# A two-layer graph network: one tile of gathered rows in each round is fetched row by row by SyncE and ScalarE

## The reference, cut to what matters

```python
def _L0_gnn_ref(feat, W1, W2, b, src, dst):
    t1 = feat @ W1
    msg = t1[src] + feat[src] * feat[dst] @ W2
    msg = msg / (sqrt(out_deg[src]) * sqrt(out_deg[dst]))[:, None]
    agg = segment_sum(msg, dst)
    embed = leaky_relu(where(in_cnt[:, None] > 0, t1 + agg, 0) + b, 0.01)
    return embed / maximum(norm(embed), 1e-12)

def _L1_gnn_ref(x, W, b, edge_index):
    xt = einsum('ni,oi->no', x, W) + b
    return segment_sum(xt[src], tgt) / (deg + 1.0)[:, None]

x = _layernorm(x + _L0_gnn_ref(x, W1, W2, b0, src, dst))
x = _layernorm(x + _L1_gnn_ref(x, W, b1, edge_index))
```

## Time and profile before

| | |
|---|---|
| median of three runs | 3954.75 us |
| the profiled execution, its span | 3955.7 us |
| GpSimd busy | 2958.4 us (75%) |
| TensorE busy, by overlapping records | 3009.0 us (76%) |
| VectorE busy | 1854.3 us (47%) |
| ScalarE busy | 671.9 us (17%) |
| layer 0, first to last gather's start | 372.2 to 1979.4 us |
| layer 1, first to last gather's start | 2004.5 to 3935.1 us |

### The profile page before, as it was taken

How to read it: one execution, slowest core, us unless ns; L and a number is a source line. 1 busy time by engine, 2 the same in 40 slices (tenths; PEclk the granted TensorE clock), 3 DMA queues, 4 the chain that set the end, 5 groups by cost and what they waited for, 6 DMA issues and landing times.

```text
span 3955.7 us, 56274 instructions
## 1 busy us (share of the span) xinstructions
PE 3009.0 (76%) x10186; PEld 1878.7 (47%) x10186; DVE 1854.3 (47%) x3529; ACT 671.9 (17%) x2118; POOL 2958.4 (75%) x3112
## 2 busy tenths in 40 slices
PE   4551887888877778788877888878788878877787
PEld 4441565655556656566534344434444434433443
DVE  9994455555555555555432323233333233323333
ACT  8991111111111111111100000000000000000000
POOL 7776777777777777777757777777777777777776
PEclk5555788888888888887857666677767777677767
DMA  7878455555555555555434444444444444444443
GB/s 254 269 236 318 134 159 158 155 159 160 156 158 158 160 156 160 157 165 157 135 89 118 121 123 122 122 122 122 121 121 121 123 122 121 121 122 122 122 121 107
DMA packets 306368, 588.12 MB, mean 149 GB/s; under 512 B 65107, under 2 KB 189178, under 8 KB 306170
## 3 DMA queue, kind: packets, MB, share of 16 engines
q0 software_dynamic: 148416, 405.47, 35.1%
q1 hardware_dynamic: 144986, 168.09, 12.7%
q10 hardware_dynamic: 12768, 12.85, 0.9%
HBM read 506.24 MB, written 75.45 MB: 147 GB/s over the span
## 4 chain that ended last, share of the span: by engine, by line
POOL 66%; issue 23%; POOLq 1%; DMA 1%; DVE 0%; DVEq 0%; PE 0%; ACT 0%; SPq 0%; ACTq 0%
POOL ring L585 66%; POOLq L582 0%; DMA ring<-scaled_x,idx 0%; DVEq L808 0%; DMA ring<-x,idx 0%; POOLq L583 0%; PE banks L1264 0%; POOL ring L595 0%; DMA x<-out_t 0%; DVE stats L1039 0%; POOLq L627 0%; DMA result<-out_t 0%; DVE out_t L1051 0%; ACT scal L738 0%; POOLq L96 0%
## 5 line engine op out<-in xcount | busy, mean ns | idle before, releaser
L1264 PE MATMUL banks<-ring,hot_space 128*128 128x257 f32 x6252 | 2399.0, 512 | 728.3 <-DMA ring<-x,idx 363.4
L1264 PEld LDWEIGHTS banks<-ring,hot_space 128*128 128x128 f32 x6252 | 1298.5, 238 | 1744.6 <-DMA ring<-x,idx 966.8
L585 POOL DMA_INDIRECT ring<-x,idx x1540 | 1462.1, 949 | 493.7 <-issue 469.2
L585 POOL DMA_INDIRECT ring<-scaled_x,idx x1270 | 1221.2, 962 | 396.5 <-issue 393.7
L970 DVE SCALAR_TENSOR_TENSOR big<-banks,here_mask,big 128x257 f32 x784 | 343.3, 479 | 1693.6 <-PE banks L1264 1693.6
L926 DVE TENSOR_TENSOR hot_space<-banks,dst_rel 128x1024 f32<-128x1024 f32 x392 | 479.6, 1225 | 181.8 <-issue 180.0
L708 ACT COPY idx<-src_col 128x8 int32 (+1 forms) x392 | 77.2, 197 | 2238.8 <-PE banks L1264 2238.8
L595 POOL DMA_INDIRECT ring<-in_x,src_col x276 | 264.9, 960 | 84.1 <-issue 84.1
L671 ACT ACTIVATE dst_rel<-columns,halves 128x128 bf16<-128x128 f32 x960 | 268.3, 375 | 4.6 <-DVE halves L843 4.6
L1163 PE MATMUL banks<-hot_space 128*128 128x98 bf16 x1088 | 101.2, 282 | 132.2 <-DVE hot_space L815 132.2
L1229 PE MATMUL banks<-w_s,a_t 128*128 128x256 f32 x784 | 195.7, 406 | 0.0
(11 more groups left out here) (121 smaller groups left out, 1169.6 us busy)
## 6 DMA issues: line engine op xcount, KB each, us to landing
src_lo<-x SPq DMA_DIRECT2D x2944, 1.0 KB
kept_rows<-ring SPq DMA_DIRECT2D x94, 384.0 KB, 3.2
ring<-kept_rows SPq DMA_DIRECT2D x47, 768.0 KB, 6.0
ring<-x,idx POOLq DMA_INDIRECT x1540, 2.8
src_lo<-scaled_x SPq DMA_DIRECT2D x1408, 1.0 KB
ring<-scaled_x,idx POOLq DMA_INDIRECT x1270, 2.8
dst_col<-in_src SPq DMA_DIRECT2D x47, 384.0 KB, 6.7
scaled_x<-big ACTq DMA_DIRECT2D x14, 896.0 KB, 17.3
```

The source lines that it names most:

```text
L585: g.indirect_dma_start(ring[:, u, 0:D], None, table[layer], bass.IndirectOffsetOnAxis(ap=idx[:, u:u + 1], axis=0)).then_inc(rows_in[u], 16)
L1264: last = nc.tensor.matmul(group_sum(k % SUMS), dst_hot[:, k % HOTS, u - k * GT, :], ring[:, u, 0:DW], start=u == tiles[0], stop=u == tiles ...
```

## The change

Both layers now treat the rounds 2 to 47 alike: GpSimd leaves out the last tile in each of them, 92 times in all where it was 34. SyncE fetches the tile of the even rounds (2h) and ScalarE that of the odd ones (2h+1), 23 each in a layer, each over the two rounds before. SyncE's two parts of 32 rows a round now stand one behind the other, ahead of the loads and stores. ScalarE gets in each round 24, 24 and 16 rows (`ACT_ROWS`), behind the index copies 0, 1 and 2 and, for the first, behind the roots; in every second round it hands the tile over after `scale_kept`. The 48 x 128 source numbers that this needs are loaded once, VectorE shifts them to byte offsets, and they are stored in `row_bytes`. The row's DMA then takes the register as it is, from the table seen as bytes.

```diff
-HANDS = (ROUNDS - 1) // 2
-SPAN = 4
-FEW = (ROUNDS - 1) // SPAN - 1
+HANDS = (ROUNDS - 3) // 2
 HAND_U = U - 1
 HAND_ROWS = 32
+ACT_ROWS = (24, 24, 16)
+ROW_BYTES = 4 * D
...
+        def one_row(layer, start):
+            return table[layer].bitcast(U8).rearrange("n (a b) -> a (n b)", a=1)[:, bass.ds(start, ROW_BYTES)]
...
+            sp.dma_start(hand_sources, src[0:(ROUNDS - 1) * U * P].rearrange("(i t e) -> i t e", t=U, e=P)[:, HAND_U, :]
+                         ).then_inc(sources_in, 16)
...
+            sp.wait_ge(ints_made, 2)
+            sp.dma_start(row_bytes, hand_sources).then_inc(ints_stored, 16)
...
             def load_hand_src(layer, h):
-                i = 2 * h + 1 if layer else SPAN * h
-                sp.dma_start(hand_src, src[bass.ds((i * U + HAND_U) * P, P)].rearrange("(a n) -> a n", a=1)
-                             ).then_inc(hand_src_in, 16)
+                sp.dma_start(hand_src[0], row_bytes[bass.ds(2 * h, 1), :]).then_inc(hand_src_in[0], 16)
...
-                for n, row in enumerate(rows):
-                    sp.dma_start(hand_rows[first + n:first + n + 1, :],
-                                 table[layer][bass.ds(row, 1), :]).then_inc(hand_in[layer], 16)
+                for n, start in enumerate(starts):
+                    sp.dma_start(hand_rows[0][first + n:first + n + 1, :].bitcast(U8),
+                                 one_row(layer, start)).then_inc(hand_in[0][layer], 16)
...
                 if hand is not None:
-                    if part == 0:
+                    if half == 0:
                         hand_free(layer, hand - 1)
-                    hand_part(layer, hand, part, load_next)
+                    hand_part(layer, hand, 2 * half)
+                    hand_part(layer, hand, 2 * half + 1, load_next)
                 next_pair(layer, i - 1)
...
+                    with g.Fori(LOOP_FIRST, ROUNDS - 1) as i:
+                        for q in range(4):
+                            gather_quarter(layer, i, q, HAND_U, 0 if layer else KEPT)
...
+            def hand_part(layer, hand, half, q, load_next):     # on ScalarE
+                if half == 0 and q == 0:
+                    act.wait_ge(hand_src_in[1], 16 * hand_no(layer, h))
+                    act.wait_ge(hand_over[1], 16 * (hand_no(layer, h) - 1))
+                first = half * P // 2 + sum(ACT_ROWS[:q])
+                _, starts = nc.values_load_multi_w_load_instructions(
+                    hand_src[1][:, first:first + ACT_ROWS[q]], engines=[mybir.EngineType.Activation], ...)
+                for n, start in enumerate(starts):
+                    nc.scalar.dma_start(hand_rows[1][first + n:first + n + 1, :].bitcast(U8),
+                                        one_row(layer, start)).then_inc(hand_in[1][layer], 16)
...
+            def pass_hand(layer, h):                             # on ScalarE
+                act.wait_ge(hand_in[1][layer], 16 * P * h)
+                act.wait_ge(groups_done, group_no(layer, 2 * h, GR - 1) + 1)
+                nc.scalar.dma_start(ring[:, HAND_U, 0:D], hand_rows[1].bitcast(F32)).then_inc(hand_over[1], 16)
...
                 if with_kept:
                     scale_kept(i)
+                if passed is not None:
+                    pass_hand(layer, passed)
                 for q in range(4):
...
                     refill(layer, i, q)
                     if ended and q == 0:
                         roots(layer, i - 2)
+                    if hand is not None and q < len(ACT_ROWS):
+                        hand_part(layer, hand, half, q, half == 1 and q == len(ACT_ROWS) - 1 and ...)
...
-                    with act.Fori(2, ROUNDS - 1) as i:
-                        round_(layer, i, True, True, layer == 0)
+                    with act.Fori(1, HANDS) as h:
+                        round_(layer, 2 * h, True, True, layer == 0, hand=h, half=1)
+                        round_(layer, 2 * h + 1, True, True, layer == 0, hand=h + 1, passed=h)
...
+            nc.vector.tensor_scalar(hand_sources, hand_sources, ROW_BYTES.bit_length() - 1, None,
+                                    ALU.logical_shift_left).then_inc(ints_made, 1)
```

More of the change, by code:

```diff
@@ new lines, in _ @@
+                    hand_part(layer, 1, 0)
+                    hand_part(layer, 1, 1)
+                    middle_round(layer, 1, with_kept, with_kept, 1, 1, True)
+                    pass_hand(layer, 1)
+                    with sp.Fori(1, HANDS - 1) as h:
+                        middle_round(layer, 2 * h, with_kept, with_kept, h + 1, 0)
+                        middle_round(layer, 2 * h + 1, with_kept, with_kept, h + 1, 1, True)
+                        pass_hand(layer, h + 1)
+                    middle_round(layer, 2 * HANDS - 2, with_kept, with_kept, HANDS, 0)
@@ L749, in scale_kept, with load_hand_src, hand_part, round_ @@
                 last.then_inc(kept_scaled, 1)
-            def round_(layer, i, sums, ended, with_kept=False, last=False):
+            def load_hand_src(layer, h):
+                nc.scalar.dma_start(hand_src[1], row_bytes[bass.ds(2 * h + 1, 1), :]).then_inc(hand_src_in[1], 16)
+            def hand_part(layer, h, half, q, load_next):
+                if half == 0 and q == 0:
+                    act.wait_ge(hand_src_in[1], 16 * hand_no(layer, h))
+                    act.sem_inc(act_turn, 1)
+                    act.wait_ge(hand_over[1], 16 * (hand_no(layer, h) - 1))
+                    act.sem_inc(act_turn, 1)
+                first = half * P // 2 + sum(ACT_ROWS[:q])
+                _, starts = nc.values_load_multi_w_load_instructions(
+                    hand_src[1][:, first:first + ACT_ROWS[q]], engines=[mybir.EngineType.Activation], min_val=0,
+                    max_val=(NODES - 1) * ROW_BYTES,
+                    skip_runtime_bounds_check_because="a source is a node's number, as for the gathers")
+                if load_next:
+                    load_hand_src(layer, h + 1)
+                for n, start in enumerate(starts):
[3 more added lines that the diff above has]
+                act.wait_ge(hand_in[1][layer], 16 * P * h)
+                act.sem_inc(act_turn, 1)
+                act.wait_ge(groups_done, group_no(layer, 2 * h, GR - 1) + 1)
+                act.sem_inc(act_turn, 1)
+                nc.scalar.dma_start(ring[:, HAND_U, 0:D], hand_rows[1].bitcast(F32)).then_inc(hand_over[1], 16)
+            def round_(layer, i, sums, ended, with_kept=False, last=False, hand=None, half=0, passed=None):
                 if with_kept:
                     scale_kept(i)
+                if passed is not None:
+                    pass_hand(layer, passed)
                 for q in range(4):
@@ L765, in round_ @@
                         roots(layer, i - 2)
+                    if hand is not None and q < len(ACT_ROWS):
+                        hand_part(layer, hand, half, q, half == 1 and q == len(ACT_ROWS) - 1
+                                  and not (isinstance(hand, int) and hand == HANDS))
             act.wait_ge(flag_made, 1)
@@ L1238, in find_places, with round_ @@
                 last.then_inc(places_found, 1)
-            def round_(layer, i, finish, end=U, with_kept=False, find=False, last_one=False):
+            def round_(layer, i, finish, end=U, with_kept=False, find=False, last_one=False, over=None, h=0):
                 for k in range(GR):
```

138 lines of the change are left out of this document (50 added, 88 removed).

## The result

The changed kernel takes **4450.7 us**, the median of four runs (4449.22 to 4453.37), where the kernel before took 3955.48 us beside it: a ratio of 1.1253, 95% interval 1.1239 to 1.1266. It is 495 us slower. The forecast was 4715 us, in a range of 4250 to 5050.

What follows compares the result with a forecast made beforehand. GpSimd's gathers bound the kernel before; the change was to shift the bound to a closed loop through ScalarE's in-order queue. 3956 + 621 (layer 0) + 138 (layer 1) = 4715 us, range 4250 to 5050.

Steps and rivals of the forecast that it cites:

- index copy 3 to copy 0: ScalarE's layer 0 loop: scaling the kept tiles and TensorE's first group, 7.3 us before clock, hand-over and jump.
- copy 0 to the second root: ScalarE's layer 0 loop: existing waits for VectorE around the roots, which nothing makes shorter, 7.0 us.
- reads, 64 rows, copies 1 and 2 and the clearing: ScalarE's layer 0 loop: offset reads 4.4 us, row issue 21.8 us, copies and clearing 0.5 us.
- `a_t` to copy 3: End of ScalarE's layer 0 loop: two a_t copies and the step to copy 3, 1.4 us.
- A row's cost: ScalarE's queue: issuing one row with byte offsets takes 0.34 us, bounds 0.27 and 0.415 us.
- the first rival: ScalarE's queue keeps up and GpSimd stays the bound: 3883 us, needing 0.16 us a row; chance 0.09.
- the second, 0.17 to 0.26: Rows on ScalarE cost 0.17 to 0.26 us, so it bounds layer 0 alone: 4060 us at 0.22; chance 0.05.
- the clock's price: Layer 0: after TensorE's idle wait, products and first group run at a lower clock, 2.5 us a round, bounds 0 to 5.7.
- Hand-over and jump: ScalarE's loop: hand-over DMA with waits, offset load and loop jump back add 1.2 us a round.
- Layer 1, +138 us: ScalarE's loop makes a layer 1 round 42.5 us against 39.5, over 46 rounds; round bounds 38.9 and 45.2.
- SyncE's load: SyncE's own work, 61 us per pair of layer 0 rounds, stays covered by ScalarE's 92 us.
- That issuers hinder each other: Rival: two issuers hinder each other or offsets gain nothing, 0.415 us a row: 5157 us; chance 0.05.

Runs made afterwards that it cites:

- the run with 32 rows: The changed kernel with ScalarE issuing 32 rows a round (16, 8, 8) in place of 64, half its tiles' rows left stale: 3894.93 us.
- the run with layer 1 alone: The changed kernel with ScalarE's tiles in layer 1 only, SyncE's tiles kept in both layers: 3906.49 us, ratio 0.9895 to the kernel before.
- the run with its tiles alone: The changed kernel without ScalarE's rows in both layers; SyncE keeps its 46 tiles, GpSimd gathers the odd rounds' tiles: 3937.11 us, ratio 0.9965.

## Why the prediction was right, and where its sum was too high

**The mechanism held.** ScalarE's loop bounds layer 0, for the reasons given. Step by step, forecast against the round shown above:
- index copy 3 to copy 0: 7.3 us, which is 11.0 with 2.5 for the clock and 1.2 for hand-over and jump; measured 9.07.
- copy 0 to the second root: 7.0 us; measured 6.89.
- reads, 64 rows, copies 1 and 2 and the clearing: 4.4 + 21.8 + 0.5 = 26.7 us; measured from 1223.96 to 1251.17, 27.2.
- `a_t` to copy 3: 1.4; measured 0.96.

**A row's cost was right.** (8.02 - 0.23) / 23 = 0.339 us against 0.34. The line of the rows, as in the earlier trace rows, and that of the reads, as in the earlier trace rows:

```profile
L750 ACTq MOVE src_lo<-scaled_x x2944: 29/29/41, 426.8 to 2448.9; - x197
L750 ACTq DMA_DIRECT2D src_lo<-scaled_x x2944: 229/230/603, 426.9 to 2449.0; - x197
```

```profile
L743 ACTq TENSOR_LOAD <-between x276: 1178/1659/1697, 425.1 to 4357.1; - x138
```

The MOVE stays, the arithmetic is gone, and ScalarE issues at SyncE's pace, though no row of before showed it doing so. Reads are 1.66 and 1.2 us for 24 and 16 numbers, forecast 1.6 and 1.2 from a line between two points. The Trainium skill gives in "DMA: Bandwidth & Descriptors", section "Anatomy of one DMA — SWDGE (gpsimd) path", about 50 ns for the sequencer's dispatch of a DMA that GpSimd issues; at that pace the 64 rows of a round would be issued in an estimated 3 us. ScalarE's queue doesn't go by it: the DMA instruction alone takes 230 ns here. The 0.34 us a row decide against the first rival, which needed 0.16, and against the second, 0.17 to 0.26.

**TensorE's idle time was right, the clock's price a little high.** Some 14 us of waiting for `a_t` were forecast and 14.37 measured. The close hit is partly luck: the forecast had TensorE's last group over 27 us after index copy 3 and the `a_t` copies at 41.0 us, and they came at 29.4 and 43.2. The products behind it took 2.2 us longer, the first group nothing (3.63 us), and copy 3 to copy 0 grew by 1.8 us. The term was 2.5. The windows of just the products and just the group show the granted clock (the last figures but two):

```profile
1251.80:1257.60 5.80, 5.79 (x17) 4.79 (x18) 0.00 (x0) 2.94 (x8) 4.43 (x5) 0.63 0.40 105
1257.60:1261.00 3.40, 3.40 (x18) 2.97 (x17) 0.00 (x0) 0.00 (x0) 2.49 (x4) 1.00 0.35 103
```

It was 0.63 of full over the products, so most of their time at the lower of the two levels, and 1.00 over the group. Over the whole window of layer 0 it fell from 0.84 to 0.77.

**Hand-over and jump, 1.2 us a round, were mis-sized:** they hide. In the round shown, with the hand-over DMA at 1211.63, copy 0 waits 6.47 us for TensorE's group all the same; copy 3 to copy 0 is 9.07 us there and 9.2 in the next round without one. The cost had been put on the path although TensorE's group lay beside it in the same step. And the jump, taken over from SyncE's 2.9 us, isn't there at all in layer 0: ScalarE's next instruction comes 0.20 to 0.23 us after the branch in each of its 21 jumps. Together with the clock and `a_t`, and less the 0.5 us by which reads and rows took longer, this is the 46.1 - 44.4 = 1.7 us a round, 78 of the 105 us between the 621 forecast for layer 0 and the 516 measured; the other 27 lie outside the steady rounds.

**Layer 1, +138 us, was the wrong step.** Its sum took copy 3 to copy 0 at 8.5 us, "and I keep 8.5":

```profile
3004.07 0.21 ACT L688 COPY idx<-src_col 128x8 int32 x1
3009.77 0.20 ACT L688 COPY idx<-src_col 128x8 int32 x1 [5.49 <-PE banks L1285]
3015.09 0.29 ACT L718 ACTIVATE scal<-mv,epsilon 128x2 f32<-128x2 f32 x1 [5.13 <-DVEq L830]
3016.86 8.14 ACTq L750 DMA_DIRECT2D src_lo<-x  x24
...
3042.99 0.21 ACT L688 COPY idx<-src_col 128x8 int32 x1
```

It is 5.7 us. The prediction itself said that the 8.5 was partly a wait for gathered rows and that 4.8 us would remain at full clock; a wait that the change makes vanish was kept in the sum as a guard against the clock. The window's clock rose from 0.72 to 0.75 instead. Without that and the 1.2 for hand-over and jump the working gives 42.5 - 2.8 - 1.2 = 38.5 us, under GpSimd's 38.9, and the round is 38.9. So layer 1 gained 24 us where it should lose 138: 162 us too much, which with the 105 of layer 0 makes the 267 us between forecast and span. The lower bound given for it, "38.9 (GpSimd takes over)", is what happened. (The jump does cost ScalarE time in layer 1, 2.65 us at the median, but it lies under the 5.49 us of waiting for the group.)

**What was hidden.** SyncE's load was put at 61 us a pair of rounds, covered. By the timelines it is some 64: the prediction charged ScalarE with a jump, but not SyncE, whose jump takes 3.2 us in the run with 32 rows. In the change that costs nothing, beneath ScalarE's 89 us; in the kernels without ScalarE's rows in layer 0 it is level with GpSimd.

**Two slips in the working.** Eight tiles in 3.71 us are 0.46 us a tile, not 0.43. The upper bound of a round in layer 1 comes to 44.8 us by its own terms (10 + 5.3 + 26.2 + 0.5 + 0.8, and 2.0 for pass and jump), not 45.2. Neither moves the forecast.

**The rivals.** That issuers hinder each other is refuted by the run with layer 1 alone and by the row's 0.339 us with both queues at work. That ScalarE keeps up is wrong for layer 0 and right, just so, for layer 1.

## What to carry to other kernels

Idle time of an in-order queue is room only where the queue waits, not behind it: add up the loop from one instruction to the same one a round later, waits included, and see whether the new work lies under a wait or extends the loop. Take out of the sum the waits that the change itself makes vanish, and don't add to it what lies beside a wait that stays. The same 64 rows a round cost nothing in one layer, 12 us in the other, and 3.7 us there when over a third of them were laid into the waits.

## What the runs showed of the hardware

- A read of numbers into registers on ScalarE takes 0.72 us for 8, 1.2 us for 16, 1.42 to 1.49 us for 20 and 1.66 us for 24. Started at byte 72 or 328, it takes 4.07 and 4.30 us for 18, where 18 from byte 0 or 256 take 1.65. All other starts here, 32, 64, 80, 144 and 304 among them, are multiples of 16 and show no such price. No run separates a rule of 16 bytes from another that these starts meet.
- A DMA of one row whose source stands in a register costs its queue 0.33 to 0.34 us on ScalarE as on SyncE; 0.403 us with the address worked out for each on ScalarE, 0.415 on SyncE before. Two streams at once don't slow each other: SyncE's rows stand 0.328 us apart in the run with its tiles alone and 0.330 in the change, beside ScalarE's (means over 184 batches of 32).
- TensorE, after 14.4 us of waiting in layer 0, took 5.83 us for products that take 3.62 us, and 3.63 us for the group right behind: the granted clock was 0.63 over the one and 1.00 over the other, so what this wait cost was 2.2 us, over within the first 16 matmuls.
- The jump back of a loop, from the branch to the queue's next instruction, took ScalarE 0.20 us in layer 0 and 2.65 us in layer 1 of the changed kernel, SyncE 2.58 and 0.24 us (medians over 21 to 23 jumps). Both of ScalarE's loops hold two rounds, so that a loop is long doesn't alone decide; no run shows what does.
